# Graph attention with explicit softmax weights, three split products per block over one table of normalised x, and W folded into the GRU weights

## The reference

```python
h = layernorm(x)
Wh = h @ W
e = leaky_relu(Wh @ a[:F] + (Wh @ a[F:]).T, 0.2)
att = softmax(where(adj > 0, e, -9e15), axis=1)
h_prime = att @ Wh
gi, gh = h_prime @ w_ih.T + b_ih, h @ w_hh.T + b_hh      # each 4096 x 768
r, z = sigmoid(i_r + h_r), sigmoid(i_z + h_z)
n = tanh(i_n + r * h_n)
x = x + (1 - z) * n + z * h
# then x = x + the experts' output: gate, top 2 of 16, silu(x w1_e) * (x w2_e) @ w3_e on layernorm(x)
```

## Time and profile before

| | |
|---|---|
| median of 3 runs | 1377.35 us (1371.50 to 1383.42) |
| the profiled execution | 1370.29 us, of which the span of its instructions is 1368.6 us |
| busy: TensorE, DVE, ScalarE, GpSimd | 1267.8, 1065.1, 671.5, 330.8 us |
| mean granted TensorE clock | 0.968 of full speed |
| first instruction of `accumulate`, last | 107.28 us, 864.4 us |

### The profile page before, as it was taken

How to read it: one execution, slowest core, us unless ns; L and a number is a source line. 1 busy time by engine, 2 the same in 40 slices (tenths; PEclk the granted TensorE clock), 3 DMA queues, 4 the chain that set the end, 5 groups by cost and what they waited for, 6 DMA issues and landing times.

```text
span 1368.6 us, 30563 instructions
## 1 busy us (share of the span) xinstructions
PE 1267.8 (93%) x8305; PEld 1101.5 (80%) x8307; DVE 1065.1 (78%) x2513; ACT 671.5 (49%) x1281; POOL 330.8 (24%) x345
## 2 busy tenths in 40 slices
PE   4668999999999999999999999637999999999995
PEld 2447989898998989899898989536888888888884
DVE  3876688787878878787887878597888888887883
ACT  3554444344444534444444444204666666666662
POOL 1011101111111011111101110004655544555554
PEclk9988999999999999999999999857999999999998
DMA  4123334333333333333343432023343455545430
GB/s 135 55 58 48 57 56 67 54 59 67 57 62 57 69 51 60 66 58 63 56 69 50 63 64 36 27 88 94 48 112 78 94 146 126 133 97 133 93 51 8
DMA packets 61970, 98.00 MB, mean 72 GB/s; under 512 B 9856, under 2 KB 36480, under 8 KB 61920
## 3 DMA queue, kind: packets, MB, share of 16 engines
q0 software_dynamic: 33600, 52.49, 25.8%
q1 hardware_dynamic: 27536, 44.14, 10.0%
q10 hardware_dynamic: 784, 0.79, 0.2%
HBM read 213.18 MB, written 18.81 MB: 170 GB/s over the span
## 4 chain that ended last, share of the span: by engine, by line
PE 83%; DMA 6%; DVE 5%; issue 3%; ACT 1%; DVEq 1%; POOL 1%; POOLq 0%; SPq 0%; ACTq 0%
PE bank L1079 37%; PE bank L1187 13%; PE bank L1201 8%; PE bank L1101 8%; PE bank L1013 6%; DMA out<-ysc,cidx 5%; PE pT L1066 4%; PE bank L1104 4%; PE bank L1120 1%; PE bank L1039 1%; ACT V L516 1%; DVE lane_hot L934 1%; POOL rstd L428 1%; DVE slot_hot L938 1%; DMA scr<-in_L_gnn_w_ih 0%
## 5 line engine op out<-in xcount | busy, mean ns | idle before, releaser
L1079 PE MATMUL bank<-V,mask 128*128 128x258 f32 x4096 | 558.4, 289 | 1.7 <-DVE comb L767 1.0
L1079 PEld LDWEIGHTS bank<-V,mask 128*128 128x128 f32 x4096 | 511.4, 190 | 2.1 <-issue 1.1
L533 ACT ACTIVATE mask<-pT 128x512 fp32r<-128x512 bf16 x512 | 277.9, 597 | 195.4 <-PE pT L1066 195.4
L1187 PE MATMUL bank<-wup,xT 128*128 128x512 f32 x948 | 239.0, 401 | 0.9 <-DVE xT L960 0.9
L1187 PEld LDWEIGHTS bank<-wup,xT 128*128 128x128 f32 x948 | 174.1, 190 | 35.0 <-DVE xT L960 1.3
L955 DVE TENSOR_TENSOR wup<-wexp,wup 128x1024 fp32r<-128x1024 f32 x158 | 185.9, 1218 | 2.2 <-ACT wup L488 1.1
L407 POOL DMA_DIRECT2D adjb<-in_adj x128 | 69.4, 542 | 479.3 <-DVE tbuf L750 455.1
L468 POOL DMA_INDIRECT out<-ysc,cidx x79 | 138.3, 1750 | 174.6 <-DMA out<-ysc,cidx 88.8
L488 ACT ACTIVATE wup<-wexp 128x1024 fp32r x158 | 165.7, 1050 | 9.7 <-DMA wexp<-in_L_ffn_w 9.2
L745 DVE CUSTOM_DVE_ANT_0 gbuf<-Dp,adjb 128x1024 bf16<-128x1024 f32 x128 | 156.3, 1221 | 4.0 <-DVE tbuf L750 0.7
L1201 PE MATMUL bank<-wexp,hidT 128*128 x632 | 150.0, 380 | 2.0 <-DVE ysc L993 1.1
(11 more groups left out here) (148 smaller groups left out, 1327.1 us busy)
## 6 DMA issues: line engine op xcount, KB each, us to landing
...
adjb<-in_adj POOLq DMA_DIRECT2D x128, 256.0 KB, 4.3
...
xg<-token_rows,gidx POOLq DMA_INDIRECT x79, 3.5
out<-ysc,cidx POOLq DMA_INDIRECT x79, 3.8
```

The lines of the kernel that those rows point to most:

```text
L533: ins = nc.scalar.activation(mask[:, c % 2, k, :], pT[c % 2][:, 0:MC], ACT.Relu, scale=sign)
L1079: ins = mm(acc[:, 0:VW], mask[:, c % 2, k, b * P:(b + 1) * P], V[:, j, 2 * k + part, :], start=j == 0 and part == 0, stop=j == T - 1 and p ...
L1187: ins = mm(acc[:, 0:HID], xT[:, r % WR, a, k * P:(k + 1) * P], wup[:, r % 2, n, b, k * HID:(k + 1) * HID], start=(k, a, b) == terms[0], st ...
```

## The change

The attention weights are now made explicitly. For each row tile ScalarE makes the logits of all 4096 columns from `Dp` with the row's term as bias (`logits`, a Relu: leaky_relu(e) = 0.2 e + 0.8 relu(e), and of the linear part the row's term cancels in the softmax while the column's is a factor exp(0.2 d_j) in the table). DVE subtracts 1 from adj (`less_one`) and adds it to the logits while it takes the row maximum (`mask_logits`), and ScalarE takes the exponential (`weights`). TensorE transposes the fp32 weights, ScalarE rounds a chunk to fp32r (`chunk_hi`), DVE takes the rest (`chunk_lo`), and `accumulate` does high x high, high x low and low x high with one table: 3 products for each block. That table is normalised x times exp(0.2 d_j), not Wh; W is multiplied into the GRU's input weights once, at the start.

All loops over tiles are written out. The value pass goes in groups of 4 tiles (`statistics`, `normalise`, `scale_values` on DVE, `value_hi` on ScalarE, `value_lo` on GpSimd). x comes in transfers of 4 tiles, and adj is loaded two tiles ahead. The transposed chunks rotate through three PSUM banks, the accumulator alternates between two. `transpose_x2` now stands before `gru` in TensorE's body and shares the bank `tp` with `transpose_h`, which moved from after chunk 2 to after chunk 3. Parts not shown: the loads and their semaphores, the transposes and products of the value pass and of the weights (`transpose_xn`, `source_term`, `target_terms`, and `weights_step` in 13 steps at tiles 5 to 17), and the same GRU and gate steps with other indices.

```diff
-        V = sb("V", [P, T, 4, VW], F32R, gs)
+        V = sb("V", [P, T, 2, VW], F32R, gs)
         Dp = sb("Dp", [P, N], F32, gs)
+        E = sb("E", [P, 2, N], F32, gs)
...
+        pc = sb("pc", [P, 3, 2, MC], F32R, gs)
...
+            def value_lo(g):
+                pool.wait_ge(s_hi, g + 1)
+                nc.gpsimd.tensor_tensor(V[:, g * 4:g * 4 + 4, 1, 0:F], xb[:, g % 2, :, :],
+                                        V[:, g * 4:g * 4 + 4, 0, 0:F].bitcast(F32), ALU.subtract).then_inc(s_lo, 1)
...
+            def value_scale(g):
+                act.wait_ge(s_sd, g + 1)
+                nc.scalar.activation(bD[:, g * 4:g * 4 + 4], accs[g % 2][:, 1:8:2], ACT.Exp, scale=SLOPE).then_inc(s_b, 1)
+            def value_hi(g):
+                act.wait_ge(s_xb1, g + 1)
+                act_copy(V[:, g * 4:g * 4 + 4, 0, 0:F], xb[:, g % 2, :, :]).then_inc(s_hi, 1)
+            def target_terms(g):
+                act.wait_ge(s_db, g + 1)
+                nc.scalar.activation(Dp[:, g * MC:(g + 1) * MC], pT[1 + g % 2][:, :], ACT.Copy, scale=REST * LSC).then_inc(s_dpe, 1)
...
+            def logits(n, q):
+                cols = slice(q * HC, (q + 1) * HC)
...
+                    act.wait_ge(s_tr, (n - 1) * CPT)
+                nc.scalar.activation(E[:, n % 2, cols], Dp[:, cols], ACT.Relu, bias=sS[:, n:n + 1]).then_inc(s_pre, 1)
+            def weights(n, q):
+                cols = slice(q * HC, (q + 1) * HC)
+                act.wait_ge(s_nmx, n + 1)
+                nc.scalar.activation(E[:, n % 2, cols], E[:, n % 2, cols], ACT.Exp, scale=1.0 / LSC,
+                                     bias=nmu[:, n % 2, 0:1]).then_inc(s_ex, 1)
+            def chunk_hi(C):
...
                 act.wait_ge(s_tr, C + 1)
-                if st is None or st * CPT + c >= 2:
-                    act.wait_ge(s_mm, C - 1)
...
+                if C >= 3:
+                    act.wait_ge(s_mm, C - 2)
+                act_copy(pc[:, C % 3, 0, :], pT[C % 3][:, :]).then_inc(s_ph, 1)
+            for q in range(Q):
+                logits(0, q)
+            value_hi(NG - 1)
+            act_copy(V[:, :, 0, F], bD[:, :]).then_inc(s_vh, 1)
...
+            def body(i):
+                if live(i, 3):
+                    act.wait_ge(s_t2, i - 2)
+                    act_copy(xn2T[:, :, :].rearrange("p k m -> p (k m)"), tp[:, 0:F]).then_inc(s_t2e, 1)
+                if i + 1 < T:
+                    for q in range(Q):
+                        logits(i + 1, q)
                 for c in range(CPT):
...
+                    if live(i, 0):
+                        chunk_hi(i * CPT + c + 2)
+                    if 1 <= c < 1 + Q and i + 1 < T:
+                        weights(i + 1, c - 1)
+                    if c == 2 and live(i, 2):
+                        rz_tanh(i)
+                    if c == 5 and live(i, 1):
+                        copy_hT(i)
+                    if c == 4 and live(i, 2):
+                        n_tanh(i)
+                    if c == 4 and live(i, 3):
...
+            def normalise(g):
+                dve.wait_ge(s_rs1, g + 1)
+                if g >= 2:
+                    dve.wait_ge(s_xb1, g - 1)
+                for r in range(4):
+                    t = g * 4 + r
+                    if g >= 2:
+                        dve.wait_ge(s_xt, t - 7)
+                    V_.tensor_scalar(xnb[:, t % 8, :], xs[:, g % 4 * 4 + r, :], xmv[:, t, 0:1], rstd[:, t:t + 1], ALU.subtract,
+                                     ALU.mult).then_inc(s_xn, 1)
...
+            def scale_values(g):
+                dve.wait_ge(s_b, g + 1)
...
+                for r in range(4):
+                    t = g * 4 + r
+                    ins = V_.tensor_scalar(xb[:, g % 2, r, :], xnb[:, t % 8, :], bD[:, t:t + 1], None, ALU.mult)
+                ins.then_inc(s_xb1, 1)
...
+            for g in range(1, NG):
+                if g + 1 < NG:
+                    statistics(g + 1)
+                normalise(g)
+                scale_values(g - 1)
+            scale_values(NG - 1)
...
+            def less_one(n, q):
+                dve.wait_ge(s_adj[q], n * 16 + 16)
+                V_.tensor_scalar(adjb[:, q, :], adjb[:, q, :], 1.0, None, ALU.subtract).then_inc(s_am, 1)
+            def mask_logits(n, q):
                 cols = slice(q * HC, (q + 1) * HC)
...
+                dve.wait_ge(s_am, n * Q + q + 1)
+                dve.wait_ge(s_pre, n * Q + q + 1)
+                V_.tensor_tensor_reduce(out=E[:, n % 2, cols], in0=E[:, n % 2, cols], in1=adjb[:, q, :], scale=1.0,
+                                        scalar=-1e30, op0=ALU.add, op1=ALU.max,
+                                        accum_out=dmx[:, n % 2, q:q + 1]).then_inc(s_ms, 1)
+            def row_max(n):
...
+                dve.wait_ge(s_ms, (n + 1) * Q)
+                if n >= 2:
+                    dve.wait_ge(s_ex, (n - 1) * Q)
+                link(V_.tensor_reduce(mxr[:, u, :], dmx[:, u, :], AX.X, ALU.max))
+                V_.tensor_scalar(nmu[:, u, :], mxr[:, u, :], -1.0 / LSC, None, ALU.mult).then_inc(s_nmx, 1)
+            def chunk_lo(C):
+                if C >= T * CPT:
+                    return
+                dve.wait_ge(s_ph, C + 1)
+                V_.tensor_tensor(pc[:, C % 3, 1, :], pT[C % 3][:, :], pc[:, C % 3, 0, :].bitcast(F32),
+                                 ALU.subtract).then_inc(s_plo, 1)
+            def combine(n):
+                dve.wait_ge(s_mm, (n + 1) * CPT)
+                acc = accs[n % 2]
+                link(V_.reciprocal(rden[:, :], acc[:, F:F + 1]))
+                if n >= 1:
+                    dve.wait_ge(s_th, n)
+                V_.tensor_scalar(hp, acc[:, 0:F], rden[:, 0:1], None, ALU.mult).then_inc(s_hp, 1)
...
+            def body(i):
+                ahead = i + 1 < T
+                if ahead:
+                    less_one(i + 1, 0)
+                    less_one(i + 1, 1)
+                if live(i, 1):
+                    combine(i - 1)
+                    remake_xn(i - 1)
+                if ahead:
+                    mask_logits(i + 1, 0)
+                    less_one(i + 1, 2)
+                    mask_logits(i + 1, 1)
+                    less_one(i + 1, 3)
+                    mask_logits(i + 1, 2)
+                for c in range(CPT):
+                    if live(i, 0):
+                        chunk_lo(i * CPT + c + 2)
+                    if c == 0 and ahead:
+                        mask_logits(i + 1, 3)
+                        row_max(i + 1)
+                    if c == 1 and live(i, 2):
+                        gru_logits(i)
+                    if c == 2 and live(i, 3):
+                        route_top(i)
+                    if c == 3 and live(i, 2):
+                        gru_n(i)
+                    if c == 4 and live(i, 3):
+                        route_weights(i)
+                    if c == 5 and live(i, 2):
+                        gru_out(i)
+                    if c == 6 and live(i, 2):
+                        norm2(i)
...
+            def transpose_weights(C):
+                if C >= T * CPT:
+                    return
+                i, c = C // CPT, C % CPT
+                if c % 2 == 0:
+                    pe.wait_ge(s_ex, i * Q + c // 2 + 1)
+                if C >= 3:
...
                 for b in range(JB):
                     j = c * JB + b
-                    for k, acc in enumerate((accp, accm)):
-                        for part in range(2):
-                            ins = mm(acc[:, 0:VW], mask[:, c % 2, k, b * P:(b + 1) * P], V[:, j, 2 * k + part, :],
-                                     start=j == 0 and part == 0, stop=j == T - 1 and part == 1)
+                    ins = tr(pT[C % 3][:, b * P:(b + 1) * P], E[:, i % 2, j * P:(j + 1) * P])
+                ins.then_inc(s_tr, 1)
+            def accumulate(i, c):
+                C = i * CPT + c
+                acc = accs[i % 2]
+                pe.wait_ge(s_plo, C + 1)
+                if c == 0 and i >= 2:
+                    pe.wait_ge(s_hp, i - 1)
+                for b in range(JB):
+                    j = c * JB + b
+                    hi, lo = (pc[:, C % 3, k, b * P:(b + 1) * P] for k in range(2))
+                    mm(acc[:, 0:VW], hi, V[:, j, 0, :], start=j == 0, stop=False)
+                    mm(acc[:, 0:VW], hi, V[:, j, 1, :], start=False, stop=False)
+                    ins = mm(acc[:, 0:VW], lo, V[:, j, 0, :], start=False, stop=j == T - 1)
                 ins.then_inc(s_mm, 1)
...
+            def transpose_x2(i):
                 pe.wait_ge(s_ln2, i - 2)
-                if after(st, 3, 1):
+                if live(i, 2):
+                    pe.wait_ge(s_hT, i - 1)
...
+            def body(i):
+                if live(i, 3):
+                    transpose_x2(i)
+                if live(i, 2):
+                    gru(i)
+                if live(i, 3) and not live(i, 0):
                     gate(i)
                 for c in range(CPT):
-                    if live(st, 0):
```

(15 more changed lines are left out.)

733 lines of the change are left out of this document (319 added, 414 removed).

## The result

The changed kernel takes 1320.8 us, median of 4 runs (1314.59 to 1322.15), beside 1374.8 for the kernel before on the same chip: the ratio is 0.959 [0.953, 0.965]. The profiled execution is 1322.15 us, its span 1320.4. The forecast was 1305 us.

| stretch, us | before | forecast | after |
|---|---|---|---|
| start to the first products of a row tile | 107.3 | 73 | 116.6 |
| graph pass, to the last product | 757.1 | 713.6 | 690.6 |
| drain, to the first product of the routing | 25.1 | 30.4 | 35.5 |
| routing and experts | 479.1 | 479.1 | 477.7 |
| span | 1368.6 | 1296 | 1320.4 |

What follows compares the result with a forecast made beforehand. In the graph pass TensorE's own list was taken to set the time. Span: 1368.6 - 34 (value pass) - 43.5 (graph pass) + 5.3 (drain) = 1296 us; against the median, 1377.35 - 72.2 = 1305 us, range 1276 to 1348.

Steps and rivals of the forecast that it cites:

- TensorE after: Graph pass: a chunk takes 1.95 us on TensorE, a row tile 21.8 us, 2.1 less; the floor of the period.
- DVE after: Graph pass, per row tile: DVE's list comes to 20.4 us without a wait, 9.0 of it side work with gaps.
- What waits for what: Graph pass: gru and all chunks queue behind norm2; period 22.6 us, TensorE stands 0.8 us per tile; pass 43.5 us less.
- The value pass: Start to first products of a row tile: 73 us against 107.3, 34 less; ends 61 and 80.
- the loop of 4.1 + L: Value pass, third xn to next group's third: 4.1 us plus L, GpSimd's value_lo subtraction, taken as 2.1; period 6.2 us.
- the value pass isn't shortened: Rival, value pass: the loop through GpSimd costs what is saved; 34 us more, 1339 us; chance 0.07.
- The drain: Behind the graph pass: the last GRU now stands behind the gate's transposes, which wait for norm2; 5.3 us more of 25.1.
- TensorE alone: Rival, graph pass: DVE's two waits vanish, TensorE alone sets a 21.8 us period; 24 us less, 1281; chance 0.13.
- DVE over: Rival, graph pass: DVE sets a 24.0 us period, less_one 0.75 us, mask_logits slower; 42 us more, 1347; chance 0.15.
- slower through `less_one`: Rival, graph pass: less_one at one column a cycle, 1.2 us; period 25.6 us; 90 us more, 1395; chance 0.06.
- The mechanism of the shared port: Rival, value pass: value_lo's L adds to DVE's 4.8 us; a group 6.9 us, kernel 1309, or 1315 at L = 3; chance 0.04.
- its signs: What would show the forecast in a trace; among them, a clock under 1.00 in the graph pass would upset the sum.

Runs made afterwards that it cites:

- the distance of the products: Kernel before, a chunk's 16 products reordered: 8 into the first accumulator, then 8 into the second, not two and two in turn; 1372.4 us, ratio 0.998.
- two-product kernel: Changed kernel without the product of the weights' high half and the table's low half, two products per block instead of three; 1374.9 us, ratio to before 1.002.

## Why the prediction was right and wrong

That the total came within 16 us is luck. Two errors of opposite sign met: the graph pass was 23 us shorter than forecast, and the value pass 44 us longer. With the drain, 5 longer, the span missed by 24 us (1320.4 against 1296). Most of the 8 us between the two misses is the starting point: the forecast was counted from a median that lay 7 us above the execution whose rows it used.

**TensorE after: right in its mechanism, the size a little high.** The list sets the time, at the full clock. A chunk is 1.88 us and not 1.95: its four fp32 transposes take 0.35 and not 0.44, since they are 0.09 each and not 0.11, while the products take 1.53 and not 1.51, the error of the mean named under the distance of the products. The floor of 21.8 us is 21.27, as the order with the GRU first shows.

**DVE after: not the bound, as forecast, and shorter.** Of the 21.87 us DVE waits 2.58 in four places (0.69 and 0.47 for ScalarE's rounding, 0.74 for the gate's exponential, 0.68 for GpSimd), which leaves 19.3 against 20.4. By start times `mask_logits` is 1.15 and `less_one` 0.33, where I had 1.22 and 0.41: four of each are 0.6 us less in a tile. The other 0.5 is side work. `less_one` lasts 0.420 us where I had 0.49. The estimate by the Trainium skill, VectorE: DVE Perf Modes, section on the perf-mode tier table, was 0.42, and the trace agrees with it.

**What waits for what: right.** TensorE waits for `norm2` in each row tile, 0.40 us in place of 0.8, and nearly never for `pc` (3.5 us in all). The order of TensorE's body costs 0.6 us a tile, by the run that undoes it. The period is 21.87 and not 22.6, from the shorter lists of TensorE and DVE: 30 tiles give 22 of the 23 us.

**The value pass: the step that failed is the loop of 4.1 + L, 6.2 us per group.** From the start of `value_hi` to the next `normalise` it was nearly right: 4.55 us in the group shown against 4.2, with L at 2.35 (taken 2.1). From the start of `normalise` to `value_hi` it had 2.0 and the group shown has 6.58. Three things were missing. First, TensorE's list is in order, and between a group's first and third transposes stand a `source_term` and the `target_terms` of the group before, at least 0.5 and 1.8 us. Second, I priced TensorE at the full clock in a stretch in which it waits, though the earlier trace rows already had 0.93 for the old value pass. The stretch with the loop intact has 44.3 us of TensorE's work at 0.75 where the one without it (the subtraction on DVE) has 33.8 at 1.00. That is 10.5 of the 29.3 us between them, the rest is standing. Third, I took the loop as one thing and never added up TensorE's own floor, 33.8 us for the five groups. The forecast for them, 5 times 6.2 and 3, was 34. That it is near the floor is chance, as it was added up from another loop; with `deviation` issued early the five groups take 37.7 us, with the subtraction on DVE 35.2.

Counted from the end of the second group's `normalise` (18.1, forecast 16.1), the six groups behind took 69 us where 40 were forecast: 29 us of the miss, with 2 ahead of them. Behind the last `normalise` come 13.6 more (29.3 us against 15.7). The forecast's own terms, 16.1, 40.2 and 15.7, add up to 72, and the 73 was 1 us over them. Of the 13.6, 8.8 are TensorE's: its last transposes, source and target terms took 12.0 us, to 99.3, where 3.2 were forecast. They ran at the lower of the clock's two levels (0.50 from 86.4 to 99.4), and `target_terms` stands there twice. Two `mask_logits` were stretched by 0.8 and 2.1 us.

**The rival "the value pass isn't shortened" came true** in its place: the loop through GpSimd costs what is saved. Its price was too small, 34 us over the forecast where 44 were measured, since the pass even grew by 9.3. It had a chance of 0.07, too low, as the forecast of 34 us rested on a loop with no row for its largest term and no list of TensorE's work.

**The drain: the size was low.** The GRU behind the gate's transposes costs 6.2 us by the run that undoes it (5.3 forecast). The other 4 of the 10.4 are in the steps around: with the GRU first, one GRU starts 9.9 us behind the other (787.73 and 797.61) where it was 7.8 before, and the second takes 5.40 us in its first part at the lower clock against 3.70. Why the transposes of h come later there wasn't tried.

**The other rivals.** TensorE alone at 21.8 us gave the period that was measured, 21.87, but not its sum: TensorE's list is 21.27 us, and its wait and order cost the other 0.6. DVE over, and slower through `less_one`: not so, by 19.3 and 0.42 us. The mechanism of the shared port is seen in the rows, at some 7 us for the kernel: the four stretched instructions with `deviation` issued early (two `normalise`, two `mask_logits`) are 6.9 us over their usual time, and the first products come at 89.4 there and at 82.2 with the subtraction on DVE. That is as cheap as the forecast had it. What no rival named is the clock in the graph pass, which the prediction had only among its signs. The two-product kernel, with 2.5 us more of waiting per tile, lost all that the change had gained.
